# Issuing every TensorE product as four products of 32 output columns

## The chip, the core and the metric

The kernel runs on one core of a Trainium2 chip. The metric is the device time of the program in microseconds (us). Two runs of the kernel before gave 811.21 and 811.91 us, median 811.56 us. TensorE is PE in the profile, its weight loads are PEld, VectorE is DVE, ScalarE is ACT, GpSimd is POOL, SyncE is SP.

## What is computed

Eight sequences of 512 tokens with 128 features pass through one transformer-like block: a layer norm modulated by a condition, two recurrences over the 512 tokens (a small state space with a silu, and a gated recurrent unit), a second layer norm, and a mixture of eight experts of which each token uses one.

```python
def step(carry, inp):                      # 512 times, one after the other
    h_ssm, h_rnn = carry
    bxt, dxt, gxt, iht = inp
    h_ssm = jax.nn.silu(h_ssm @ A.T + bxt)
    y_ssm = h_ssm @ Cw.T + Cb + dxt
    hh = h_rnn @ W_hh.T + b_hh
    i_r, i_z, i_n = jnp.split(iht, 3, axis=-1)
    h_r, h_z, h_n = jnp.split(hh, 3, axis=-1)
    r = jax.nn.sigmoid(i_r + h_r)
    z = jax.nn.sigmoid(i_z + h_z)
    n = jnp.tanh(i_n + r * h_n)
    h_rnn = (1.0 - z) * n + z * h_rnn
    y_rnn = h_rnn @ proj_w.T + proj_b
    fused = gxt[:, :1] * y_ssm + gxt[:, 1:2] * y_rnn
    return ((h_ssm, h_rnn), fused)
...
for e in range(8):                         # expert of a token: argmax of its gate
    ye = jax.nn.relu(x @ w1[e] + b1[e]) @ w2[e] + b2[e]
    out = out + jnp.where(expert_idx == e, ye * expert_w, 0.0)
```

Everything is float32, apart from a few exact bfloat16 helpers (counts of tokens per expert, and the bias of the output in three bfloat16 parts).

## The kernel before

The features lie on the 128 partitions. The 512 tokens of a sequence are 512 steps; 16 steps of the eight sequences make a tile of 128 tokens, so there are 32 tiles. Each engine has one long program, written out step by step in Python (`steps`, up to U_END), and the engines meet through semaphores; nothing reorders the work at run time apart from these waits.

A step g on TensorE (`step`, L1276) is, in this order: the product of W_hh for r with the state h (L1287, 16 moving columns of which 8 are used), the one for n (L1291, 32 columns), the one for z (L1296, 16 columns). I call these three the narrow products. Then comes what the step has of the tile's other work (`tile_work`, L1232: output, router, token counts, input products), up to two units of the experts (`unit`, L1182), or, where a step has room, a product whose result nobody reads (`hold_clock`, L1177, 128 or 256 columns), and last the product of the state space (L1168, widened to 128 columns, of which 8 are used). I call all with 128 or more moving columns wide. In the 512 steps there are 1536 narrow products, 1237 wide float32 products of 128 (or 130) columns, 62 of 256, 113 transposes, 62 bfloat16 products of 128 columns and 31 of 258 (the bias); behind the last step there are 200 wide products and 16 transposes more, for the last tile and the remaining experts.

The first narrow product waits for h (`h_ready`), which is on every other engine's path: ACT takes the sigmoid of r from PSUM (L685), DVE forms i_n + r * h_n as a scan (L1015, waits for r's sigmoid and for n's product), ACT takes the tanh (L709), DVE forms the new h with another scan (L1023), and h_ready goes up again.

In float32 each product is issued as two passes of a weight load and a matmul (the trace has 1024 of each for 512 products); a transpose is one pass. The bias product L1241 has three rows (`ones_tok = ones_bf[0:KB, :]`, KB = 3), all others 128.

Of the kernel before, what the change touches and what calls it, by code (L numbers as in the profile page):

```python
# [17 lines left out]
BF16 = mybir.dt.bfloat16  # L18
I32 = mybir.dt.int32
U32 = mybir.dt.uint32  # L20
ALU = mybir.AluOpType
# [3 lines left out]
P = 128  # L25
# [6 lines left out]
EPS = 1e-5  # L32
BANK = 512
R_WIDE, N_WIDE, Z_WIDE, S_WIDE = 16, 32, 16, 128
HW = 32


KB = 3
# [50 lines left out]
RING = 12  # L89
# [117 lines left out]
def adaln_kernel(nc, x, silu_in, weights, ssm_weights, w1, b1, w2, b2, col_bias, bias_a, bias_b,  # L207
                 bias_const, const, out):
    ctx = ExitStack()
    with ctx:  # L210
# [27 lines left out]
        part_b = sb("part_b", [KB, BI_ALL], BF16)  # L238
        bias_bf = sb("bias_bf", [KB, BI_ALL], BF16)
        ones_bf = sb("ones_bf", [P, P], BF16)  # L240
# [211 lines left out]
        ident = const_sb[:, C_ID:C_ID + P]  # L452
        ones_tok = ones_bf[0:KB, :]

# [87 lines left out]
        def _(eng):  # L542
# [7 lines left out]
            eng.memset(s_ring[:, 1, T - 1, :], 0.0).then_inc(state_zeroed, 1)  # L550
            eng.memset(s_ring[:, 0, :, :], 0.0).then_inc(state_zeroed, 1)
            nc.gpsimd.iota(order_i[:, :], [[1, P]], base=0, channel_multiplier=-1).then_inc(iota_set, 1)
            nc.gpsimd.iota(count_i[:, :], [[1, 16]], base=0, channel_multiplier=0).then_inc(iota_set, 1)
# [216 lines left out]
        def _(eng):  # L770
# [83 lines left out]
            nc.vector.memset(ones_e[:, :], 1.0).then_inc(tables_set, 1)  # L854
            eng.wait_ge(state_zeroed, 7)

            def bias_part(n):


                if n == 0:  # L860
                    eng.wait_ge(bias_loaded, 48)
                    nc.vector.tensor_tensor(part_f[:, :], ba_sb[:, :], bb_sb[:, :], ALU.add).then_inc(bias_step, 1)
                    return
                eng.wait_ge(bias_step, n)
                k, what = divmod(n - 1, 3)
                mask = bc_sb[:, k:k + 1]
                if what == 0:
                    nc.vector.tensor_copy(part_b[:, :], part_f[:, :]).then_inc(bias_step, 1)
                if what == 1 and k == 0:
                    nc.vector.tensor_scalar(bias_bf[:, :], part_b[:, :], mask, None, ALU.mult).then_inc(bias_step, 1)  # L870
                if what == 1 and k > 0:
                    nc.vector.scalar_tensor_tensor(out=bias_bf[:, :], in0=part_b[:, :], scalar=mask,
                                                   in1=bias_bf[:, :], op0=ALU.mult, op1=ALU.add).then_inc(bias_step, 1)
                if what == 2:
                    nc.vector.tensor_tensor(part_f[:, :], part_f[:, :], part_b[:, :],
                                            ALU.subtract).then_inc(bias_step, 1)
# [241 lines left out]
        def _(eng):  # L1118
            mm = nc.tensor.matmul

# [14 lines left out]
            def pre(j, q, part):  # L1135

                if part == 0:
                    ge(eng, h1_ready, j + 1)
                    nc.tensor.transpose(work[:, 0:P], h1[:, :], ident).then_inc(h1T_filled, 1)
                if part == 1:  # L1140
# [21 lines left out]
            for part in range(1, 5):  # L1162
                pre(0, 0, part)
            eng.wait_ge(state_zeroed, 7)

# [16 lines left out]
            def unit(kind, i, second):  # L1182
# [6 lines left out]
                if kind == "X":  # L1189
# [7 lines left out]
                    else:  # L1197
                        ge(eng, h_ready, NT * T)
                    nc.tensor.transpose(rows_bank(n), xs_sb[:, b, :], ident).then_inc(x_filled, 1)  # L1199
                    return  # L1200
# [31 lines left out]
            def tile_work(c, q, t, g):  # L1232
# [3 lines left out]
                if exists(j):  # L1236
# [14 lines left out]
                    if t == 9:  # L1251
                        ge(eng, h2_ready, j + 1)
                        if exists(c + 1):
                            ge(eng, h1T_ready, c + 2)
                        nc.tensor.transpose(work[:, 0:P], h2_ring[:, j % RING, :], ident).then_inc(h2T_filled, 1)
                    if t == 10:
# [122 lines left out]
```

## Time and profile before

| | |
|---|---|
| time, median of 2 runs | 811.56 us |
| the profiled execution, its span | 825.0 us |
| PE busy, PEld busy | 799.6 us (97%), 754.8 us (91%) |
| DVE, ACT, POOL busy | 447.4, 388.8, 128.0 us |
| passes on PE | 6316 |
| granted TensorE clock, mean | 0.987 |

All terms of the prediction are made against the profiled execution, whose span is 13.4 us longer than the median. A busy PE is one with a matmul record open; such records overlap and their ends are modelled, so that PE's 97% doesn't tell whether PE is what the others wait for. The groups of rows further down show the step at close range.

### The profile page before, as it was taken

How to read it: one execution, taken by the hardware profiler on the slowest of the kernel's cores; microseconds unless marked ns; L12 is line 12 of the kernel's file. 1: busy time of each engine (PE TensorE's matmuls, PEld its weight loads, DVE VectorE, ACT ScalarE, POOL GpSimd, SP SyncE). 2: the span in 40 equal slices, each digit the busy share in tenths (PEclk: the TensorE clock that was granted, in tenths of full speed). 3: DMA queues.
4: the chain of work that ended last, by engine and by line, in shares of the span. 5: the costliest groups of instructions: out<-in, count | busy, mean ns of one | idle time of the engine just before them, and what ended most of it. 6: DMA issues, size and time to landing. Idle time of an engine off the chain costs nothing.

```text
span 825.0 us, 20239 instructions
## 1 busy us (share of the span) xinstructions
PE 799.6 (97%) x6316; PEld 754.8 (91%) x6316; DVE 447.4 (54%) x2715; ACT 388.8 (47%) x2689; POOL 128.0 (16%) x218
## 2 busy tenths in 40 slices
PE   8999999999999999999999999999999999998496
PEld 6999999999999999999999999999999999997486
DVE  5444444455555555555555556555556555656255
ACT  5444444444555444455555454555545555543132
POOL 2001111111110101111111111111111111212502
PEclk9999999999999999999999999999999999999789
DMA  8723000505322000062221002522200442215521
GB/s 315 277 86 123 6 4 5 207 6 194 108 76 71 11 11 11 25 224 106 68 67 50 11 11 78 206 81 82 81 14 18 147 140 88 84 60 208 202 64 46
DMA packets 45404, 75.72 MB, mean 92 GB/s; under 512 B 6284, under 2 KB 27090, under 8 KB 45170
## 3 DMA queue, kind: packets, MB, share of 16 engines
q1 hardware_dynamic: 41058, 68.40, 23.2%
q0 software_dynamic: 2368, 4.85, 2.1%
q10 hardware_dynamic: 1872, 1.18, 0.5%
q8 instruction: 51, 0.84, 0.4%
q14 instruction: 55, 0.45, 0.2%
HBM read 14.31 MB, written 21.04 MB: 43 GB/s over the span
## 4 chain that ended last, share of the span: by engine, by line
PE 95%; another core or an unknown queue 2%; DVE 1%; issue 1%; DMA 0%; ACT 0%; ACTq 0%; DVEq 0%
PE s_bank L1168 15%; PE nr_bank L1291 15%; PE nr_bank L1287 14%; PE z_bank L1296 13%; PE y_bank L1222 9%; PE hid_bank_b L1180 7%; PE hid_bank_a L1209 5%; PE hid_bank_b L1209 4%; PE work L1243 2%; PE nr_bank L1143 1%; PE s_bank L1155 1%; PE work L1258 1%; PE work L1246 1%; PE hid_bank_a L1199 1%; PE z_bank L1151 1%
## 5 line engine op out<-in xcount | busy, mean ns | idle before, releaser
L685 ACT ACTIVATE r_fac<-nr_bank 128x8 f32<-128x8 f32 x512 | 91.3, 178 | 280.1 <-PE nr_bank L1287 277.2
L1015 DVE TENSOR_TENSOR_SCAN nr_bank<-r_fac,nr_bank 128x16 f32<-128x16 f32 x512 | 100.0, 195 | 205.8 <-PE nr_bank L1291 201.2
L1168 PE MATMUL s_bank<-s_ring,ws_sb 128*128 128x128 f32 x1024 | 207.0, 284 | 0.0
L1291 PE MATMUL nr_bank<-h_ring,w_sb 128*128 128x32 f32 x1024 | 199.8, 279 | 0.0
L1296 PE MATMUL z_bank<-h_ring,w_sb 128*128 128x16 f32 x1024 | 191.6, 263 | 0.0
L1287 PE MATMUL nr_bank<-h_ring,w_sb 128*128 128x16 f32 x1024 | 184.9, 256 | 0.0
L1287 PEld LDWEIGHTS nr_bank<-h_ring,w_sb 128*128 128x128 f32 x1024 | 152.4, 188 | 22.2 <-DVE h_ring L1023 13.6
L1023 DVE TENSOR_TENSOR_SCAN h_ring<-z_fac,h_ring 128x24 f32<-128x24 f32 x512 | 106.5, 208 | 119.5 <-ACT h_ring L709 106.9
L1168 PEld LDWEIGHTS s_bank<-s_ring,ws_sb 128*128 128x128 f32 x1024 | 158.2, 190 | 7.1 <-issue 1.9
L1296 PEld LDWEIGHTS z_bank<-h_ring,w_sb 128*128 128x128 f32 x1024 | 155.5, 192 | 0.0
L1291 PEld LDWEIGHTS nr_bank<-h_ring,w_sb 128*128 128x128 f32 x1024 | 155.5, 192 | 0.0
L707 ACT ACTIVATE z_fac<-z_bank 128x8 f32<-128x8 f32 x512 | 92.6, 181 | 88.1 <-PE z_bank L1296 85.8
L562 POOL TENSOR_TENSOR ve<-mv,eps 128x1 f32<-128x1 f32 x64 | 12.0, 187 | 517.6 <-DVE mv L787 517.6
L709 ACT ACTIVATE h_ring<-nr_bank 128x16 f32<-128x16 f32 x512 | 92.2, 180 | 0.1
L691 ACT ACTIVATE s_fac<-s_bank 64x8 f32<-64x8 f32 x512 | 81.1, 158 | 0.4 <-PE s_bank L1168 0.4
L1180 PE MATMUL hid_bank_b<-w_sb,const_sb 128*128 128x128 f32 (+1 forms) x286 | 76.2, 348 | 0.0
L1019 DVE TENSOR_TENSOR s_ring<-s_bank,s_fac 64x8 f32<-64x8 f32 x512 | 75.6, 148 | 1.0
L1209 PE MATMUL hid_bank_a<-xT,wx 128*128 128x128 f32 x264 | 57.4, 300 | 9.5 <-issue 5.5
L678 ACT ACTIVATE hid_a<-hid_bank_a,wx 128x128 f32<-128x128 f32 x132 | 48.2, 365 | 30.6 <-PE hid_bank_a L1209 19.8
L1209 PE MATMUL hid_bank_b<-xT,wx 128*128 128x128 f32 x264 | 56.7, 298 | 2.4 <-DVE hid_b L1081 2.3
L1222 PE MATMUL y_bank<-wx,hid_a 128*128 128x128 f32 x264 | 56.2, 295 | 0.5 <-DVE y_sb L1093 0.5
L1222 PE MATMUL y_bank<-wx,hid_b 128*128 128x128 f32 x264 | 56.4, 296 | 0.0
(182 smaller groups left out, 1105.1 us busy)
## 6 DMA issues: line engine op xcount, KB each, us to landing
wx<-w_all SPq DMA_DIRECT2D x66, 578.0 KB
rows<-zeros SPq DMA_DIRECT2D x3, 4096.0 KB, 13.9
w_all<-in_w SPq DMA_DIRECT2D x2, 2048.0 KB, 15.5
xs_sb<-rows SPq DMA_DIRECT2D x54, 64.0 KB, 2.5
rows<-y_sb SPq DMA_DIRECT2D x54, 64.0 KB, 1.6
x_sb<-in_x SPq DMA_DIRECT2D x1, 1920.0 KB, 8.8
out<-o_sb SPq DMA_DIRECT2D x20, 64.0 KB
y_rows<-y_sb SPq DMA_DIRECT2D x12, 64.0 KB, 1.8
```

What stands on the lines that cost most here:

```text
L685: nc.scalar.activation(r_fac[:, t % 2, :, 1], r_cols(q, t), ACT.Sigmoid).then_inc(rn_ready, 1)
L707: nc.scalar.activation(z_fac[:, t % 2, :, 2], z_cols(g), ACT.Sigmoid).then_inc(sig_ready, 1)
L709: nc.scalar.activation(scan_data(pq, pt).rearrange("p (b m) -> p b m", m=3)[:, :, 0:3:2], n_pairs(q, t)[:, :, 1:2].to_broadcast([P, B, 2]) ...
L1015: nc.vector.tensor_tensor_scan(pairs, r_fac[:, k, :, :].rearrange("p b k -> p (b k)"), pairs, 0.0, ALU.mult, ALU.add).then_inc(pre_n_ready, 1)
L1023: nc.vector.tensor_tensor_scan(h_ring[:, q, t, 0:3 * B], z_fac[:, k, :, :].rearrange("p b m -> p (b m)"), scan_data(pq, pt), 0.0, ALU.mult ...
L1168: return mm(s_cols(g, width=S_WIDE), ws_sb[:, 0:P], s_ring[:, pq, pt, :], start=False, stop=True, skip_group_check=True)
L1180: mm(hid_bank[1][:, 0:width], ident, w_sb[:, W_MOD:W_MOD + width], start=True, stop=True)
L1209: mm(hid_bank[second][:, 0:P], w_all[:, e, at:at + P] if dense else wx1[:, b, at:at + P], h2T[:, (NT - 1) % 2, :] if dense else xT[:, n % ...
L1222: last = mm(dense_y(e) if dense else y_bank[:, 0:P], (hid_a, hid_b)[second][:, h, :], w_all[:, e, FC * P + at:FC * P + at + P] if dense el ...
L1287: mm(r_cols(q, t, R_WIDE), w_sb[:, W_HH:W_HH + P], h[:, 0:R_WIDE], start=False, stop=True, skip_group_check=True).then_inc(r_ready, 1)
L1291: mm(n_pairs(q, t, N_WIDE)[:, :, 0], w_sb[:, W_HH + 2 * P:W_HH + 3 * P], h[:, 0:N_WIDE], start=False, stop=True, skip_group_check=True).th ...
L1296: mm(z, w_sb[:, W_HH + P:W_HH + 2 * P], h[:, 0:z.shape[1]], start=False, stop=True, skip_group_check=True).then_inc(z_ready, 1)
```

## The change

TensorE's program no longer calls the matmul directly. A helper `mm` cuts the stationary operand into four pieces of 32 columns and issues four products, each into 32 partitions of the output, with the same moving operand; a semaphore is raised by the last of the four. The transposes become products of the tile (as weights) with the identity (as moving operand), through the same helper, and so have two passes per piece. The bias operand gets all 128 partitions, zero but for the first three, and the ones beside it too, so that the bias product has 128 rows as all others have. One memset on POOL at the start is added, and the waits for it.

```diff
--- before.py
+++ after.py
@@ -31,6 +31,7 @@
 FC = 4
 EPS = 1e-5
 BANK = 512
+COLS = 32
 R_WIDE, N_WIDE, Z_WIDE, S_WIDE = 16, 32, 16, 128
 HW = 32
 
@@ -236,7 +237,7 @@
         bc_sb = sb("bc_sb", [KB, KB])
         part_f = sb("part_f", [KB, BI_ALL])
         part_b = sb("part_b", [KB, BI_ALL], BF16)
-        bias_bf = sb("bias_bf", [KB, BI_ALL], BF16)
+        bias_bf = sb("bias_bf", [P, BI_ALL], BF16)
         ones_bf = sb("ones_bf", [P, P], BF16)
         ct_sb = sb("ct_sb", [P, B])
         ct_sig = sb("ct_sig", [P, B])
@@ -450,7 +451,7 @@
 
         mod_sa, mod_ca, mod_ga, mod_sb, mod_cb, mod_gb = (mod[:, k * P:(k + 1) * P] for k in range(6))
         ident = const_sb[:, C_ID:C_ID + P]
-        ones_tok = ones_bf[0:KB, :]
+        ones_tok = ones_bf[:, :]
 
         block = ctx.enter_context(nc.Block())
 
@@ -549,6 +550,7 @@
             eng.memset(z_fac[:, :, :, 1], -1.0).then_inc(state_zeroed, 1)
             eng.memset(s_ring[:, 1, T - 1, :], 0.0).then_inc(state_zeroed, 1)
             eng.memset(s_ring[:, 0, :, :], 0.0).then_inc(state_zeroed, 1)
+            eng.memset(bias_bf[:, :], 0.0).then_inc(state_zeroed, 1)
             nc.gpsimd.iota(order_i[:, :], [[1, P]], base=0, channel_multiplier=-1).then_inc(iota_set, 1)
             nc.gpsimd.iota(count_i[:, :], [[1, 16]], base=0, channel_multiplier=0).then_inc(iota_set, 1)
             nc.gpsimd.iota(block_i[:, :], [[P, E * GMAX]], base=0, channel_multiplier=0).then_inc(iota_set, 1)
@@ -852,7 +854,7 @@
                                            op0=ALU.add, op1=ALU.mult).then_inc(mod_ready, 1)
             nc.vector.memset(ones_bf[:, :], 1.0).then_inc(ones_set, 1)
             nc.vector.memset(ones_e[:, :], 1.0).then_inc(tables_set, 1)
-            eng.wait_ge(state_zeroed, 7)
+            eng.wait_ge(state_zeroed, 8)
 
             def bias_part(n):
 
@@ -867,10 +869,10 @@
                 if what == 0:
                     nc.vector.tensor_copy(part_b[:, :], part_f[:, :]).then_inc(bias_step, 1)
                 if what == 1 and k == 0:
-                    nc.vector.tensor_scalar(bias_bf[:, :], part_b[:, :], mask, None, ALU.mult).then_inc(bias_step, 1)
+                    nc.vector.tensor_scalar(bias_bf[0:KB, :], part_b[:, :], mask, None, ALU.mult).then_inc(bias_step, 1)
                 if what == 1 and k > 0:
-                    nc.vector.scalar_tensor_tensor(out=bias_bf[:, :], in0=part_b[:, :], scalar=mask,
-                                                   in1=bias_bf[:, :], op0=ALU.mult, op1=ALU.add).then_inc(bias_step, 1)
+                    nc.vector.scalar_tensor_tensor(out=bias_bf[0:KB, :], in0=part_b[:, :], scalar=mask,
+                                                   in1=bias_bf[0:KB, :], op0=ALU.mult, op1=ALU.add).then_inc(bias_step, 1)
                 if what == 2:
                     nc.vector.tensor_tensor(part_f[:, :], part_f[:, :], part_b[:, :],
                                             ALU.subtract).then_inc(bias_step, 1)
@@ -1116,7 +1118,16 @@
 
         @block.tensor
         def _(eng):
-            mm = nc.tensor.matmul
+            def mm(out, weights, moving, start, stop, skip_group_check=False):
+
+                for c in range(0, P, COLS):
+                    last = nc.tensor.matmul(out[c:c + COLS], weights[:, c:c + COLS], moving, start=start, stop=stop,
+                                            skip_group_check=skip_group_check)
+                return last
+
+            def transpose(out, tile):
+
+                return mm(out, tile, ident, start=True, stop=True)
 
 
             def fill(filled):
@@ -1136,7 +1147,7 @@
 
                 if part == 0:
                     ge(eng, h1_ready, j + 1)
-                    nc.tensor.transpose(work[:, 0:P], h1[:, :], ident).then_inc(h1T_filled, 1)
+                    transpose(work[:, 0:P], h1[:, :]).then_inc(h1T_filled, 1)
                 if part == 1:
                     ge(eng, n_seeded, 2 * j + 2)
                     ge(eng, h1T_ready, j + 1)
@@ -1161,7 +1172,7 @@
             eng.wait_ge(w_loaded, 48)
             for part in range(1, 5):
                 pre(0, 0, part)
-            eng.wait_ge(state_zeroed, 7)
+            eng.wait_ge(state_zeroed, 8)
 
             def state_space(g, pq, pt):
 
@@ -1196,7 +1207,7 @@
                         ge(eng, relu_a_ready, 2 * i)
                     else:
                         ge(eng, h_ready, NT * T)
-                    nc.tensor.transpose(rows_bank(n), xs_sb[:, b, :], ident).then_inc(x_filled, 1)
+                    transpose(rows_bank(n), xs_sb[:, b, :]).then_inc(x_filled, 1)
                     return
                 if kind in "AC":
                     if kind == "A" and not second:
@@ -1252,7 +1263,7 @@
                         ge(eng, h2_ready, j + 1)
                         if exists(c + 1):
                             ge(eng, h1T_ready, c + 2)
-                        nc.tensor.transpose(work[:, 0:P], h2_ring[:, j % RING, :], ident).then_inc(h2T_filled, 1)
+                        transpose(work[:, 0:P], h2_ring[:, j % RING, :]).then_inc(h2T_filled, 1)
                     if t == 10:
                         ge(eng, h2T_ready, j + 1)
                         mm(work[:, 0:P], h2T[:, jq, :], repeated(w_sb[:, W_ROUTE:W_ROUTE + E]),
```

What stands on PE's queue, in the order of the program. First, the second step of the second tile and most of the third, as an example of the loop: h_ring is the state h, nr_bank and z_bank take the gates, hid_bank_b takes the product that keeps the clock or an expert's hidden layer, s_bank the state space. Before:

```order
L1287 MATMUL nr_bank<-h_ring,w_sb 128x16
L1291 MATMUL nr_bank<-h_ring,w_sb 128x32
L1296 MATMUL z_bank<-h_ring,w_sb 128x16
L1246 MATMUL work<-w_sb,h_hist 128x128
L1249 MATMUL work<-ws_sb,s_hist 128x128
L1168 MATMUL s_bank<-s_ring,ws_sb 128x128
L1287 MATMUL nr_bank<-h_ring,w_sb 128x16
L1291 MATMUL nr_bank<-h_ring,w_sb 128x32
L1296 MATMUL z_bank<-h_ring,w_sb 128x16
L1180 MATMUL hid_bank_b<-w_sb,const_sb 128x256
```

The same place with the change:

```order
L1124 MATMUL nr_bank<-h_ring,w_sb 32x16 x4
L1124 MATMUL nr_bank<-h_ring,w_sb 32x32 x4
L1124 MATMUL z_bank<-h_ring,w_sb 32x16 x4
L1124 MATMUL work<-w_sb,h_hist 32x128 x4
L1124 MATMUL work<-ws_sb,s_hist 32x128 x4
L1124 MATMUL s_bank<-s_ring,ws_sb 32x128 x4
L1124 MATMUL nr_bank<-h_ring,w_sb 32x16 x4
L1124 MATMUL nr_bank<-h_ring,w_sb 32x32 x4
L1124 MATMUL z_bank<-h_ring,w_sb 32x16 x4
L1124 MATMUL hid_bank_b<-w_sb,const_sb 32x256 x4
```

No product changes its place; each has become four in a row, all of them issued by the helper's line 1124, with 32 output partitions instead of 128 and the same number of moving columns.

The other place is the first step of that tile, where the bias product stands (bias_bf, into the bank work). Before:

```order
L1296 MATMUL z_bank<-h_ring,w_sb 128x16
L1241 MATMUL work<-bias_bf,ones_bf 128x258
L1243 MATMUL work<-w_sb,h1T 128x130
L1168 MATMUL s_bank<-s_ring,ws_sb 128x128
L1287 MATMUL nr_bank<-h_ring,w_sb 128x16
```

With the change:

```order
L1124 MATMUL z_bank<-h_ring,w_sb 32x16 x4
L1124 MATMUL work<-bias_bf,ones_bf 32x258 x4
L1124 MATMUL work<-w_sb,h1T 32x130 x4
L1124 MATMUL s_bank<-s_ring,ws_sb 32x128 x4
L1124 MATMUL nr_bank<-h_ring,w_sb 32x16 x4
```

Here too the order stays, and the bias product has 32 columns and 128 rows like its neighbours.

## Rows read from the trace of the kernel before

**Rows 1.** The page: busy time of each engine, and the granted clock over the span.

```profile
PE 799.6 (97%) x6316; PEld 754.8 (91%) x6316; DVE 447.4 (54%) x2715; ACT 388.8 (47%) x2689; POOL 128.0 (16%) x218
...
PEclk9999999999999999999999999999999999999789
```

**Rows 2.** The line that makes h: count, ns min/median/max, first and last start.

```profile
L1023 DVE TENSOR_TENSOR_SCAN h_ring<-z_fac,h_ring x512: 207/208/210, 11.4 to 743.2; 128x24 f32<-128x24 f32 x171
```

**Rows 3.** Timeline of one step, all engines: start us, us, engine, line, instruction, count.

```profile
300.30 0.21 DVE L1023 TENSOR_TENSOR_SCAN h_ring<-z_fac,h_ring 128x24 f32<-128x24 f32 x1 [0.24 <-ACT h_ring L709]
...
300.56 0.30 PEld L1287 LDWEIGHTS nr_bank<-h_ring,w_sb 128*128 128x128 f32 x2
...
300.78 0.30 PEld L1291 LDWEIGHTS nr_bank<-h_ring,w_sb 128*128 128x128 f32 x2
...
300.99 0.18 ACT L685 ACTIVATE r_fac<-nr_bank 128x8 f32<-128x8 f32 x1 [0.73 <-PE nr_bank L1287]
301.00 0.30 PEld L1296 LDWEIGHTS z_bank<-h_ring,w_sb 128*128 128x128 f32 x2
...
301.23 0.20 DVE L1015 TENSOR_TENSOR_SCAN nr_bank<-r_fac,nr_bank 128x16 f32<-128x16 f32 x1 [0.39 <-PE nr_bank L1291]
...
301.51 0.18 ACT L709 ACTIVATE h_ring<-nr_bank 128x16 f32<-128x16 f32 x1
...
301.73 0.21 DVE L1023 TENSOR_TENSOR_SCAN h_ring<-z_fac,h_ring 128x24 f32<-128x24 f32 x1 [0.24 <-ACT h_ring L709]
...
301.99 0.30 PEld L1287 LDWEIGHTS nr_bank<-h_ring,w_sb 128*128 128x128 f32 x2
```

**Rows 4.** Who waited for whom during the 512 steps: total us, times, longest.

```profile
ACT r_fac L685 <- PE nr_bank L1287: 276.4, 491, 0.8
DVE nr_bank L1015 <- PE nr_bank L1291: 200.1, 437, 0.9
...
PEld nr_bank L1287 <- DVE h_ring L1023: 13.6, 89, 0.2
```

**Rows 5.** Groups of TensorE instructions by shape: count, busy us, mean ns, idle before.

```profile
L1168 PE MATMUL s_bank<-s_ring,ws_sb 128*128 128x128 f32 x1024 | 207.0, 284 | 0.0
...
L1296 PE MATMUL z_bank<-h_ring,w_sb 128*128 128x16 f32 x1024 | 191.6, 263 | 0.0
...
L1255 PE MATMUL work<-const_sb,h_ring 128*128 128x128 f32 x32 | 9.8, 308 | 0.1
```

**Rows 6.** Timeline of weight loads around a 256-column product.

```profile
24.13 0.41 PEld L1168 LDWEIGHTS s_bank<-s_ring,ws_sb 128*128 128x128 f32 x2
```

**Rows 7.** Timeline of matmuls at the same place.

```profile
23.82 0.68 PE L1180 MATMUL hid_bank_b<-w_sb,const_sb 128*128 128x256 f32 x2
24.34 0.38 PE L1168 MATMUL s_bank<-s_ring,ws_sb 128*128 128x128 f32 x2
```

**Rows 8.** Timeline of matmuls around the two bfloat16 products of a tile.

```profile
76.78 0.22 PE L1264 MATMUL work<-onehot,before 128*128 128x128 bf16 x1
76.84 0.22 PE L1266 MATMUL work<-onehot,ones_bf 128*128 128x128 bf16 x1
76.90 0.44 PE L1180 MATMUL hid_bank_b<-w_sb,const_sb 128*128 128x128 f32 x2
```

**Rows 9.** Timeline of weight loads around the three-row bias product.

```profile
79.39 0.30 PEld L1296 LDWEIGHTS z_bank<-h_ring,w_sb 128*128 128x128 f32 x2
79.72 0.09 PEld L1241 LDWEIGHTS work<-bias_bf,ones_bf 3*128 3x128 bf16 x1
79.93 0.30 PEld L1243 LDWEIGHTS work<-w_sb,h1T 128*128 128x128 f32 x2
```

**Rows 10.** Stretches of the steps and behind them: length, busy us (count), clock.

```profile
11.40:743.20 731.80, 731.41 (x5868) 695.84 (x5868) 401.40 (x2543) 357.94 (x2602) 100.02 (x174) 1.00 0.24 85
743.20:825.00 81.80, 59.12 (x422) 54.24 (x421) 39.59 (x148) 23.23 (x72) 23.75 (x26) 0.87 0.38 131
```

**Rows 11.** The page: PE's instruction fetches, and a 64 KB transfer from issue to landing.

```profile
q8 instruction: 51, 0.84, 0.4%
...
xs_sb<-rows SPq DMA_DIRECT2D x54, 64.0 KB, 2.5
```

## The prediction

> **What bounds the kernel now.** I began with the page [rows 1]: PE has a matmul open in 97% of the span and its clock is full until the last few slices, which looks like a kernel bound by TensorE. The rest says otherwise. The line that makes h runs 512 times, first at 11.4 and last at 743.2 us [rows 2]: (743.2 - 11.4) / 511 = 1.432 us a step, in steps that hold quite different products. One step at close range [rows 3] is a ring: h's scan starts at 300.30, r's first weight load at 300.56 (0.26 later), the sigmoid of r at 300.99 (0.43), the scan for n at 301.23 (0.24), tanh at 301.51 (0.28), h's next scan at 301.73 (0.22): 1.43 us, all of it one after the other. ACT and DVE wait in it for the products of r and n, and PE's next load of r for h, if only by 13.6 us in all [rows 4].
>
> So two things have nearly the same length. The ring takes 1.43 us. PE's own work per step is six products at 0.22 us (the loads of r, n and z start at 300.56, 300.78, 301.00 [rows 3]), 1.34 us with 0.224 each. The other stretches matter less: 11.4 us before the first h, and 81.8 us behind the last, of which PE is busy 59.1 [rows 10].
>
> **What sets 0.22 us.** Products of 16 and of 128 moving columns have the same pace, two loads at 0.11 us each, so for the narrow ones the load is what counts: 0.112 for 128 weight columns. Streaming shows where 256 columns move: the next product's loads begin when the last such pass starts (24.13 [rows 6]), and its first matmul starts at 24.34 [rows 7], so 256 columns stream in 0.21 to 0.22 us and 128 in 0.109. A wide product is thus bound twice over, by loading and by streaming, at about the same 0.11 us a pass.
>
> **Loads after the change.** Four pieces of two passes make eight loads per product. In proportion to its columns a load of 32 takes 0.028 us, eight 0.224, as now. No row shows a load of fewer than 128 columns, nor two at once. The lower bound is that the four pieces load side by side, two loads in a row, 0.056 a product. The upper bound comes from the densest stream there is, the bfloat16 pair: matmuls start at 76.78, 76.84, 76.90 [rows 8], each with its load, so a load and a matmul are certainly issued every 0.056 us, 0.448 a product. I take 0.224, as the rate per column is the only thing measured. The Trainium skill, TensorEngine Tiling, section Instruction Overhead, says that each matmul costs about 60 cycles however few columns move; as an estimate from that page this is 25 ns, 0.2 us per narrow product, and the sum below would be about 37 us less. No row here decides between the two.
>
> **Streaming after the change.** This is the largest term. The moving operand isn't cut, so each of the eight passes streams all its columns: 0.109 us for 128. The lower bound is that the four pieces run fully side by side: two passes in a row, 0.22 us, as now. The upper bound is that none overlaps: 8 x 0.109 = 0.872. I take a value between, from the order on the queue. The pieces are issued one after the other, and each as its first pass, then its second. The second pass of a piece needs the same 32 columns of the array as the first, so it starts when that one has streamed. PE starts matmuls in the order of the program in all timelines read; if it keeps to that, the first pass of piece two waits behind the second of piece one, and then runs beside it. So at most two passes run at once, and a product takes four passes, 4 x 0.109 = 0.436 us. The Trainium skill, TensorE: Matmul & The Clock Gate, section The mechanism, also says that matmuls start strictly in order. The same page's table of measured speedups has three column tiles of one pass each at 2.38 times; an estimate with that, 0.872 / (4 x 0.79) = 0.276 us a wide product, would give about 850 us, but it has no second pass on the same tile, which is what I expect to block.
>
> **The sum.** In the 512 steps, by the counts of the program: 1536 narrow products x 0.224 = 344 us; wide ones, 1237 of 128 columns, 113 transposes (one pass now [rows 5], full products then) and 62 of 256 as two each, 1474 x 0.436 = 643; bfloat16 products 7. Together 994 us. No step falls below the ring: with three wide products it has 3 x 0.224 + 3 x 0.436 = 1.98 us on PE against 1.43, and steps with any other mix of the same size are alike. PE is then the bound, and ring waits vanish inside it. Now the 512 steps take 732, so +262. Behind them 200 wide products gain 0.212 each and 16 transposes 0.324, 47 us; PE's idle 22.7 us of that stretch [rows 10] are waits for other engines, and I let all 47 stand. Before the first step the wide fills and input products double, some 4 us. The span becomes 825 + 262 + 47 + 4 = 1138 us; the median stood 13.4 us below its span, so **1125 us**.
>
> Costed at nothing: the memset on POOL lies before 4 us, while POOL next waits for DVE. The bias product now makes PE pause: loads start 79.72 and 79.93 around it, the last load before at 79.50 [rows 9], some 0.2 us of idle in 31 steps, 6 us at most, and with PE the bound this is a gain that its four pieces, streaming 258 columns, eat. Instruction fetches quadruple from 51 [rows 11]; the queue runs ahead of them now without a mark in the steps. If each of some 153 new ones stood free for as long as a small transfer, 2.5 us [rows 11], that would be 380 us, but one is needed only every 5 us.
>
> If the queue order holds but narrow products reach half my price, 0.112, the steps take 172 + 643 + 7 = 822 and the time is about 950. So the likeliest case has its own range, 950 to 1190.
>
> **The rivals.**
> *Faster: the pieces run side by side.* If a blocked second pass doesn't hold up the next piece, a wide product stays at 0.224. If loads overlap too, a narrow one falls to 0.112, the wait from r's load to its sigmoid from 0.43 to 0.32, and n's product is earlier still. The ring is 0.112 shorter, PE needs 6 x 0.17 = 1.01 us, and 512 x 0.112 = 57 us go: 755 us, or 725 with loads of 0.056. For it: the ring is what counts now, and its PE part is nearly half load time. Against it: the order of the passes. It decides from the point where three narrow and three wide products fit 1.43 us; at 0.436 the wide ones alone take 1.31.
> *No change: streaming side by side, loads as now.* Narrow 0.224, wide 0.224, the ring and PE as before: about 812 us. The change then does nothing.
> *Slower through issue.* If each load with its matmul costs 0.056 us whatever its size [rows 8], every product takes 0.448: 688 + 660 + 7 in the steps, with the tail about 1490 us. Against it: that spacing is also just the streaming of 128 bfloat16 columns.
> *Much slower: no overlap at all.* Wide 0.872: steps 344 + 1285 + 7 = 1636, with the tail about 1860 us. For it: the trace shows no two matmuls of pieces at once. Against it: pieces use different columns and output partitions.
>
> **How the numbers follow.** Queue order, 1125 us (950 to 1190): 0.54. Faster, 755: 0.18. No change, 812: 0.10. Issue, 1490: 0.08. No overlap, 1860: 0.10. The range of 725 to 1200 leaves out the last two, about 2 in 10, and takes in both signs, since the bounds of the wide product decide the sign. A measurement of this kernel tells about 2% from no change. Faster by more than 2%: 0.18; within 2%: 0.10; slower: 0.72.
>
> **What would show it.** In the profile after: the state space product's eight passes spread over 0.44 us, with neighbours starting in pairs; PE without waits in the loop; and ACT's sigmoid and DVE's scans waiting longer for PE at each step, about 1.9 us from one h to the next. The narrow price shows in the starts of r, n and z: 0.22 apart if loads are proportional, 0.11 or less if they overlap. I am wrong if wide products take 0.25 us or less: then the ring decides again, and the sign with it. The tail term is wrong if the stretch behind the last h isn't about 130 us.

## The result, and the profile after

Two runs of the changed kernel took 850.01 and 859.72 us, median 854.87 us, against 811.56 before: ratio 1.053, 95% interval 1.039 to 1.068. It is slower, as forecast, and inside the range, but it loses 43 us and not 313.

The profiled execution took 850.01 us, with a span of 847.9. The page: the first line gives busy time, share of the span and instructions of each engine, the second the granted clock in 40 slices, the third PE's instruction fetches (count, MB, share of the transfer engines).

```profile
PE 706.2 (83%) x25784; PEld 466.4 (55%) x25784; DVE 446.4 (53%) x2715; ACT 405.0 (48%) x2689; POOL 127.9 (15%) x219
...
PEclk9998999899999999999999999999999999999999
...
q8 instruction: 203, 3.33, 1.6%
```

PE is less busy than before (83% against 97% [rows 1]) in a longer span. Something other than PE's work holds it. The one figure that has quadrupled along with the passes is the count of instruction fetches, 51 [rows 11] to 203. 3.33 MB over 203 fetches is 16.4 KB each. PE's queue has 2 x 25784 loads and matmuls and some 530 waits for semaphores, 52095 records in all, and over 203 that is 256.6: a fetch brings some 256 instructions. I call 256 instructions a block.

The line that makes h (L1025 now), with the times of its first and last scan:

```profile
L1025 DVE TENSOR_TENSOR_SCAN h_ring<-z_fac,h_ring x512: 207/208/210, 11.7 to 777.1; 128x24 f32<-128x24 f32 x171
```

(777.1 - 11.7) / 511 = 1.498 us a step, against 1.432 [rows 2]. That is the mean. The typical step is another matter. One step at close range (start, length, engine, line, operation, out<-in, count, idle time before it and what ended that):

```profile
311.90 0.21 DVE L1025 TENSOR_TENSOR_SCAN h_ring<-z_fac,h_ring 128x24 f32<-128x24 f32 x1 [0.20 <-ACT h_ring L711]
...
312.16 0.22 PEld L1124 LDWEIGHTS nr_bank<-h_ring,w_sb 128*32 128x32 f32 x16 [0.25 <-DVE h_ring L1025]
...
312.28 0.18 PEld L1124 LDWEIGHTS z_bank<-h_ring,w_sb 128*32 128x32 f32 x8
...
312.49 0.18 ACT L687 ACTIVATE r_fac<-nr_bank 128x8 f32<-128x8 f32 x1 [0.62 <-PE nr_bank L1124]
...
312.70 0.20 DVE L1017 TENSOR_TENSOR_SCAN nr_bank<-r_fac,nr_bank 128x16 f32<-128x16 f32 x1 [0.52 <-ACT r_fac L687]
...
312.93 0.19 ACT L711 ACTIVATE h_ring<-nr_bank 128x16 f32<-128x16 f32 x1
...
313.01 0.42 PE L1124 MATMUL s_bank<-s_ring,ws_sb 128*32 128x128 f32 x8
...
313.15 0.21 DVE L1025 TENSOR_TENSOR_SCAN h_ring<-z_fac,h_ring 128x24 f32<-128x24 f32 x1 [0.20 <-ACT h_ring L711]
```

From scan to scan it takes 1.25 us, where the ring of before took 1.43 [rows 3]. From r's load to its sigmoid it is 0.33 us (0.43 before), from the sigmoid to the scan for n 0.21 (0.24), from there to tanh 0.23 (0.28). The sixteen loads of r and n together start within 0.12 us, 0.06 a product, where one took 0.22.

The state-space product has eight passes, each with 128 moving columns. The matmuls of that product alone, in two stretches, 312.99 to 313.12 and 312.99 to 313.16 (count, shortest/median/longest ns, first and last start):

```profile
L1124 PE MATMUL s_bank<-s_ring,ws_sb x4: 297/297/297, 313.0 to 313.0; 128*32 128x128 f32 x4
...
L1124 PE MATMUL s_bank<-s_ring,ws_sb x8: 272/285/297, 313.0 to 313.2; 128*32 128x128 f32 x8
```

Four passes are under way by 313.03 and nothing more starts until after 313.13; then the other four start within 0.03 us. In the trace's single records, neighbours within each four start some 7 ns apart. So all four pieces stream at once, and a wide product costs two passes in a row, as before.

So the ring did become shorter. A typical step, by which I mean the tenth percentile of the 511 times from scan to scan, takes 1.243 us against 1.427 before; the median, 1.292, already holds delays. So 512 x 0.184 = 94 us should have gone. Here is one place where they went, weight loads a little later:

```profile
313.41 0.22 PEld L1124 LDWEIGHTS nr_bank<-h_ring,w_sb 128*32 128x32 f32 x16 [0.25 <-DVE h_ring L1025]
313.53 0.12 PEld L1124 LDWEIGHTS z_bank<-h_ring,w_sb 128*32 128x32 f32 x1
314.50 0.15 PEld L1124 LDWEIGHTS z_bank<-h_ring,w_sb 128*32 128x32 f32 x7 [0.85 <-issue]
```

One of z's eight loads goes out, and the next seven come 0.97 us later, with no semaphore behind it ("issue" is waiting for nothing the profile shows). In the transfer records an instruction fetch runs from 311.97 to 313.31, and the next starts at 315.76. The stop lies inside a product, where the program has no wait. In PE's waits (total us, times, longest) such stops are spread over all its tiles:

```profile
PEld nr_bank L1124 <- issue: 40.8, 50, 3.2
...
PEld z_bank L1124 <- issue: 28.0, 37, 4.0
...
PEld s_bank L1124 <- issue: 21.0, 34, 2.1
...
PEld hid_bank_a L1124 <- issue: 14.7, 27, 1.5
...
PEld y_bank L1124 <- issue: 10.8, 15, 1.4
...
PEld hid_bank_b L1124 <- issue: 9.8, 9, 2.1
...
PEld work L1124 <- issue: 9.1, 13, 1.5
```

These seven rows are 134 us, 124 of them in the steps. The steps together exceed 512 typical ones by 130 us; before, by 2.6. Counting PE's instructions through, waits included, 133 of its 324 gaps over 0.35 us stand at one and the same place modulo 256, and no other place has more than 5.

The single records settle what these 133 stops wait for. Blocks and fetches pair one to one, 203 and 203. At the 133 places PE goes on 1.39 us (median; nine in ten between 1.24 and 1.57) behind the end of the fetch that brings the block. The next fetch starts only after PE has entered that block, 1.04 us later at the least and 1.23 in the median. And of the 130 us, 116 lie in the 228 steps that touch the end of a block, 10 in the steps right behind these, and 4.6 in the other 95.

The two stretches, with the columns of [rows 10] (length, busy us and count of PE, PEld, DVE, ACT, POOL, clock, DMA share, GB/s):

```profile
11.70:777.10 765.40, 638.92 (x23913) 414.86 (x23916) 400.48 (x2542) 374.26 (x2601) 99.56 (x174) 0.98 0.25 84
777.10:847.90 70.80, 57.44 (x1748) 47.98 (x1745) 39.50 (x148) 23.13 (x72) 23.82 (x26) 0.94 0.45 154
```

The steps cost 765.4 - 731.8 = 33.6 us more. The rest behind them took 81.8 us in the profiled execution of before. That execution had a span of 825.0; a time lies 2.1 above its span (850.01 and 847.9), so the median of 811.56 belongs to a span of 809.4, and the profiled one was 15.6 longer. Its steps ran undisturbed at full clock and its tail at 0.87 [rows 10], so I put the 15.6 to the tail. Without them it has 66.2, and the tail becomes about 4.6 us longer with the change, an estimate. The start went from 11.4 to 11.7.

**The theory.** The pieces overlap fully, and the ring gives back 94 us. But in the steps PE now has 94.5 instructions each, 93.6 of them loads and matmuls (23.9 before), so 256 of them last 256 / 94.5 x 1.243 = 3.37 us at the ring's pace, and the next 256 take about 4 us to come. I call this *fetch*. The rival, *work*, says that the extra passes themselves, or the waits among them, make some steps longer, wherever they lie in the fetch blocks.

### The profile page after: what moved, and what is told of

The parts are those of the page before. It is cut to its first block, busy times and chain, and to the rows that moved or that the text cites. A ratio compares the mean times of both kernels' runs of the same rounds, so it can differ in the third digit from the quotient of the medians.

```text
span 847.9 us, 59176 instructions
## 1 busy us (share of the span) xinstructions
PE 706.2 (83%) x25784; PEld 466.4 (55%) x25784; DVE 446.4 (53%) x2715; ACT 405.0 (48%) x2689; POOL 127.9 (15%) x219
## 3 DMA queue, kind: packets, MB, share of 16 engines
q8 instruction: 203, 3.33, 1.6%
## 4 chain that ended last, share of the span: by engine, by line
PE 71%; issue 14%; DVE 6%; ACT 5%; DMA 1%; SPq 1%; POOL 0%; DVEq 0%; POOLq 0%
PE s_bank L1124 23%; PE nr_bank L1124 19%; PE hid_bank_b L1124 8%; PE work L1124 6%; PE y_bank L1124 6%; PE hid_bank_a L1124 5%; PE z_bank L1124 4%; ACT r_fac L687 3%; DVE nr_bank L1017 3%; DVE s_ring L1021 1%; DMA out<-o_sb 1%; ACT h_ring L711 0%; DMA xs_sb<-rows,x_index 0%; ACT s_bank L658 0%; DVE fin_g L1101 0%
## 5 line engine op out<-in xcount | busy, mean ns | idle before, releaser
L1124 PE MATMUL s_bank<-s_ring,ws_sb 128*32 128x128 f32 x4096 | 236.1, 287 | 29.6 <-DVE s_ring L1021 16.1
L1124 PE MATMUL nr_bank<-h_ring,w_sb 128*32 128x16 f32 (+1 forms) x8192 | 203.5, 202 | 31.5 <-issue 30.1
L1124 PEld LDWEIGHTS nr_bank<-h_ring,w_sb 128*32 128x32 f32 x8192 | 144.1, 112 | 114.1 <-DVE h_ring L1025 76.8
L1124 PEld LDWEIGHTS s_bank<-s_ring,ws_sb 128*32 128x32 f32 x4096 | 104.6, 110 | 140.0 <-DVE s_ring L1021 107.1
L1025 DVE TENSOR_TENSOR_SCAN h_ring<-z_fac,h_ring 128x24 f32<-128x24 f32 x512 | 106.3, 208 | 115.1 <-ACT h_ring L711 114.0
L1124 PE MATMUL z_bank<-h_ring,w_sb 128*32 128x16 f32 x4096 | 142.3, 191 | 20.4 <-issue 20.2
L1124 PEld LDWEIGHTS z_bank<-h_ring,w_sb 128*32 128x32 f32 x4096 | 106.8, 118 | 26.5 <-issue 26.5
L1124 PE MATMUL hid_bank_b<-w_sb,const_sb 128*32 128x128 f32 (+1 forms) x1144 | 79.8, 335 | 2.3 <-issue 2.3
L1124 PE MATMUL hid_bank_b<-xT,wx 128*32 128x128 f32 x1056 | 60.4, 281 | 6.1 <-issue 5.5
L1124 PE MATMUL hid_bank_a<-xT,wx 128*32 128x128 f32 x1056 | 59.9, 284 | 3.9 <-issue 3.7
L1124 PE MATMUL y_bank<-wx,hid_a 128*32 128x128 f32 x1056 | 59.7, 277 | 3.7 <-issue 3.4
L680 ACT ACTIVATE hid_a<-hid_bank_a,wx 128x128 f32<-128x128 f32 x132 | 48.0, 364 | 19.9 <-PE hid_bank_a L1124 19.5
```

The lines of the kernel that those rows point to most:

```text
L680: nc.scalar.activation(hid_a[:, h, :], hid_bank[0][:, 0:P], ACT.Relu, bias=bias1(i, 2 * h)).then_inc(relu_a_ready, 1)
L1025: nc.vector.tensor_tensor_scan(h_ring[:, q, t, 0:3 * B], z_fac[:, k, :, :].rearrange("p b m -> p (b m)"), scan_data(pq, pt), 0.0, ALU.mult ...
L1124: last = nc.tensor.matmul(out[c:c + COLS], weights[:, c:c + COLS], moving, start=start, stop=stop, skip_group_check=skip_group_check)
```

## The experiments

Numbers in the table are worked out from the h scans and from the counts of PE's instructions in the steps (loads, matmuls and 0.9 waits a step). "Typical step" is the tenth percentile of the time from scan to scan, "excess" what the steps take beyond as many typical ones, whatever the reason; "block at ring pace" is 256 / (instructions per step) x (typical step), "block measured" the time from first to last scan over the number of blocks in it.

| kernel | time, us | ratio (95%) | typical step | mean step | instr. per step | block at ring pace | block measured | excess, us |
|---|---|---|---|---|---|---|---|---|
| before | 811.56 | – | 1.427 | 1.432 | 23.9 | 15.3 | 15.4 | 3 |
| after, 32 columns | 854.87 | 1.053 (1.039–1.068) | 1.243 | 1.498 | 94.5 | 3.37 | 4.06 | 130 |
| 64 columns | 737.27 | 0.908 (0.906–0.910) | 1.263 | 1.287 | 47.7 | 6.78 | 6.91 | 12 |
| state space 2 of 4 | 805.25 | 0.992 (0.989–0.996) | 1.242 | 1.407 | 86.5 | 3.68 | 4.16 | 84 |
| narrow ones only | 772.66 | 0.950 (0.944–0.956) | 1.255 | 1.359 | 59.9 | 5.36 | 5.81 | 53 |
| 16 passes added | 964.42 | 1.192 (1.184–1.199) | 1.244 | 1.718 | 110.5 | 2.88 | 3.98 | 242 |
| zeros written later | 849.18 | 1.045 (1.043–1.047) | 1.243 | 1.512 | 94.5 | 3.37 | 4.10 | 137 |
| state space 2 of 4, no fill | 785.54 | 0.969 (0.964–0.973) | 1.242 | 1.376 | 82.1 | 3.87 | 4.29 | 68 |
| 64, lean state space | 730.52 | 0.901 (0.899–0.903) | 1.263 | 1.277 | 43.7 | 7.40 | 7.48 | 7 |

### Half as many pieces: 64 columns

```diff
-COLS = 32
+COLS = 64
```

> Pieces of 64 columns instead of 32: half the instructions of the changed kernel on PE (about 26 thousand against 52). Fetch theory (PE stops at every 256th instruction until the next block of instructions has come, about 4 us after the one before): a block then lasts over five steps, 6.9 us, no stop is left, and the ring of a step is 1.24 us plus 0.056 for the two longer loads of r, 1.30 us: 512 x 1.30 + 82 = about 750 us. Work theory (the pieces themselves cost PE time, or the clock that drops in the stops): halving the pieces takes back half of the loss, about 830 us.

737.27 us, ratio 0.908. This is the test with the most in it: the same mechanism of pieces, half the instructions. The page and PE's waits for issue:

```profile
PE 706.1 (96%) x12892; PEld 532.6 (72%) x12892; DVE 443.7 (60%) x2715; ACT 422.4 (57%) x2689; POOL 128.1 (17%) x219
...
q8 instruction: 102, 1.67, 0.9%
```

```profile
PEld s_bank L1124 <- issue: 6.0, 19, 0.3
...
PEld hid_bank_a L1124 <- issue: 5.9, 15, 0.6
...
PEld nr_bank L1124 <- issue: 2.6, 6, 0.6
```

The loss through issue is down to an eighth, 17 us in all rows, where the kernel before has 16. The typical step is only 0.02 us longer than with 32 columns, so nearly all of the ring's gain is there already. The 12 us of excess that are left aren't stops: the steps at place 5 of a tile's 16 take 1.32 us and those at 11 to 13 1.29 (medians).

### Half of the state-space pieces left out

The product of the state space writes 128 partitions, of which the state uses the first 64; the two pieces behind are left out.

```diff
-            def mm(out, weights, moving, start, stop, skip_group_check=False):
+            def mm(out, weights, moving, start, stop, skip_group_check=False, cols=P):
-                for c in range(0, P, COLS):
+                for c in range(0, cols, COLS):
...
-                          start=False, stop=True, skip_group_check=True)
+                          start=False, stop=True, skip_group_check=True, cols=SSM)
```

> The changed kernel, but the state space product (64 outputs used, 128 columns issued) issues only the two pieces whose result is read: 8 instructions less per step, 4096 in all, 16 blocks of 256; nothing that is used is left out. Fetch theory: 16 blocks x 4.05 us = about 65 us less, 790 us. Work theory: the four pieces run side by side, so two take as long as four: no change, 850 to 855 us.

805.25 us, 50 less than after. The product's pieces stream at once, so its duration is the same with two, and the typical step is indeed unchanged (1.242). What fell is the instructions, by 8 a step, 16 blocks in the steps: 50 / 16 = 3.1 us a block. That is a good deal of the 4 us expected, and nothing that *work* allows.

### Sixteen instructions added to each step

```diff
+                mm(s_cols(g), ws_sb[:, 0:P], zeros[:, 0:B], start=False, stop=True, skip_group_check=True)
                 return mm(s_cols(g, width=S_WIDE), ws_sb[:, 0:P], s_ring[:, pq, pt, :],
```

The added product adds zeros, in the stretch of the step in which PE waits for the state anyway.

> The changed kernel plus one product of 8 moving columns of zeros per step, added to the state space bank in front of its product: 16 instructions more per step, 8192 in all, 32 blocks; results are unchanged. Fetch theory: 32 x 4.05 us = 130 us more, about 985 us. Work theory: PE has 0.06 us more to do in a step in which it idles a sixth of the time: 855 to 885 us.

964.42 us, 110 more than after, for 8 matmuls of 8 columns with their loads. The typical step doesn't move (1.244). Loads and matmuls in the steps grow by 32 blocks, 3.4 us each. PE's waits:

```profile
PEld s_bank L1124 <- issue: 61.1, 75, 4.7
PEld nr_bank L1124 <- issue: 58.8, 68, 2.4
...
PEld z_bank L1124 <- issue: 38.7, 35, 3.8
```

Each of the three has grown (21.0, 40.8 and 28.0 in after), the products of r and z too, which the edit doesn't touch. The added instructions cost where the block ends, not where they stand. *Work* falls with this run and the one before.

### Only the three narrow products in pieces

Made from the kernel before, with a helper `pieces` like `mm` of the change; all other products stay whole.

```diff
-                    mm(r_cols(q, t, R_WIDE), w_sb[:, W_HH:W_HH + P], h[:, 0:R_WIDE],
+                    pieces(r_cols(q, t, R_WIDE), w_sb[:, W_HH:W_HH + P], h[:, 0:R_WIDE],
...
-                    mm(n_pairs(q, t, N_WIDE)[:, :, 0], w_sb[:, W_HH + 2 * P:W_HH + 3 * P], h[:, 0:N_WIDE],
+                    pieces(n_pairs(q, t, N_WIDE)[:, :, 0], w_sb[:, W_HH + 2 * P:W_HH + 3 * P], h[:, 0:N_WIDE],
...
-                    mm(z, w_sb[:, W_HH + P:W_HH + 2 * P], h[:, 0:z.shape[1]],
+                    pieces(z, w_sb[:, W_HH + P:W_HH + 2 * P], h[:, 0:z.shape[1]],
```

> The kernel before, with only the three narrow products of a step in four pieces; all others, transposes and the three-row bias product too, as before. 31 thousand PE instructions, so by the fetch theory no stop is left. Then what shows is the price of changing between pieces and whole products twice a step. If a change costs nothing, the ring is that of the changed kernel, 1.24 us, and the time about 720 us. If each costs 0.2 us as around the three-row bias product of before, PE needs 0.3 + 0.2 + 0.67 + 0.2 = 1.37 us a step: about 785 us, more if the second change falls on the ring.

772.66 us, ratio 0.950. The ring's gain needs only the three narrow products, and 59.9 instructions a step stay clear of the 4 us. But over a quarter of the steps take about 1.48 us, while most take 1.255, and it isn't the fetch: steps that touch the end of a block are no longer than others (medians 1.259 and 1.260). Nor is it the number of wide products, as two of three steps with three of them take about 1.26 us. 122 of the 147 steps over 1.45 us stand at places 5 and 11 to 13 of a tile. There PE has a product of the next tile beside the one of the state space (11 to 13), or the state space's product waits for its bank (5), and r's load comes 0.50 us behind the start of h's scan, where it comes 0.28 behind it in other steps. Weight loads of a usual step, and then the end of a step at place 11, with h's scan:

```profile
451.28 0.22 PEld L1125 LDWEIGHTS nr_bank<-h_ring,w_sb 128*32 128x32 f32 x16
451.40 0.18 PEld L1125 LDWEIGHTS z_bank<-h_ring,w_sb 128*32 128x32 f32 x8
451.61 0.30 PEld L1254 LDWEIGHTS work<-w_sb,h_hist 128*128 128x128 f32 x2
```

```profile
26.93 0.30 PEld L1176 LDWEIGHTS s_bank<-s_ring,ws_sb 128*128 128x128 f32 x2 [0.21 <-DVE s_ring L1020]
...
27.08 0.21 DVE L1024 TENSOR_TENSOR_SCAN h_ring<-z_fac,h_ring 128x24 f32<-128x24 f32 x1 [0.20 <-ACT h_ring L710]
27.15 0.30 PEld L1155 LDWEIGHTS nr_bank<-h1T,w_sb 128*128 128x128 f32 x2
...
27.57 0.22 PEld L1125 LDWEIGHTS nr_bank<-h_ring,w_sb 128*32 128x32 f32 x16
```

In the first, z's loads begin at 451.40 and the first whole load comes 0.21 us later, where the next product follows z's after 0.09 us when it is in pieces too (in after, 312.28 to 312.37). In the second, a whole product follows another after 0.22 us (26.93 to 27.15), but r's pieces follow a whole one after 0.42, although h's scan ended at 27.29. Each change between pieces and whole thus costs 0.1 to 0.2 us, two a step. In most steps h comes no earlier than PE is through with the change; at the four places it does, and with 64 columns, where nothing changes, the same places take 1.29 to 1.32 us instead of 1.48. These 122 steps make about 27 of the 53 us of excess; the rest I did not take apart. The Trainium skill, TensorEngine Tiling, section Key Properties, says that changing the tiling mode drains the engine; it gives no price, and the trace agrees with about 0.2 us at most a change.

### The long transfers moved

Zeros are written to two large buffers in tiles 2 and 6; here in tiles 4 and 10. Nothing else changes.

```diff
-                if t == 0 and c in (2, 6):
+                if t == 0 and c in (4, 10):
-                    zero_rows(1 if c == 2 else 2)
+                    zero_rows(1 if c == 4 else 2)
```

> The changed kernel with the two 4 MB transfers that zero row buffers moved from the start of tiles 2 and 6 to the start of tiles 4 and 10. In the changed kernel the 16 steps of tiles 2, 4, 6, 10 take 26.3, 22.4, 27.3, 23.9 us. If instruction fetches are slowed by bulk transfers, the long tiles move along: about 22, 27, 22.5, 28 us, the time unchanged, 855 us. If the long tiles have another reason (what is computed in them), they stay where they are.

849.18 us: total within what two runs of after leave open, but the long tiles have moved. Stretches of tiles 2, 4, 6 and 10 in after, with the columns of the stretches above:

```profile
63.63:89.95 26.32, 21.14 (x722) 13.88 (x719) 11.12 (x74) 10.84 (x78) 2.68 (x5) 0.87 0.46 166
...
112.45:134.86 22.41, 19.59 (x721) 11.69 (x718) 11.02 (x74) 10.78 (x78) 2.61 (x5) 1.00 0.03 7
...
156.41:183.72 27.31, 21.34 (x721) 13.97 (x718) 11.02 (x73) 10.83 (x78) 2.61 (x5) 0.88 0.43 159
...
254.71:278.62 23.91, 20.59 (x778) 13.57 (x782) 12.68 (x80) 12.21 (x85) 2.61 (x5) 1.00 0.21 71
```

And with the zeros in tiles 4 and 10:

```profile
65.06:86.83 21.77, 19.82 (x722) 11.25 (x718) 11.08 (x73) 10.81 (x78) 2.68 (x5) 1.00 0.03 8
...
108.54:133.77 25.23, 20.33 (x721) 13.12 (x719) 11.01 (x74) 11.04 (x78) 2.61 (x5) 0.93 0.47 172
...
155.88:177.50 21.62, 19.22 (x722) 12.00 (x718) 11.02 (x74) 10.72 (x78) 2.61 (x5) 1.00 0.03 7
...
248.99:280.42 31.43, 22.64 (x778) 17.43 (x775) 12.73 (x81) 12.40 (x85) 2.61 (x5) 0.84 0.53 194
```

Tile 6 goes from 27.3 to 21.6 us as its transfers leave, tile 10 from 23.9 to 31.4 as they come, with the same count of matmuls. So fetches come later where bulk transfers run. Yet a quiet tile at full clock takes 21.6 to 22.4 us, and 16 x 1.243 is 19.9: without any transfer the steps would lose some 2 us a tile, an estimate of 50 to 80 us of the 130 over 32 tiles. Inside tile 2 of after, three stretches of 5 us, one in the burst and two behind it:

```profile
70.00:75.00 5.00, 2.76 (x68) 1.64 (x61) 1.68 (x9) 1.37 (x12) 0.76 (x1) 0.81 1.02 369
75.00:80.00 5.00, 4.75 (x158) 4.13 (x161) 1.94 (x12) 1.90 (x13) 0.75 (x2) 0.66 0.06 20
80.00:85.00 5.00, 4.60 (x200) 3.00 (x192) 2.51 (x18) 2.36 (x20) 0.00 (x0) 1.00 0.03 7
```

PE gets through 68 matmuls while the transfers move 369 GB/s, and through 200 later. The granted clock falls to its lower level, 1.2 GHz, behind that starved stretch (0.66 from 75 to 80), and the two steps that start there take 1.69 and 1.60 us, the next three 1.25. The clock is thus part of the loss, and it follows the stops: the steps have 0.98 on average, against 1.00 before [rows 10]. The trace bounds its share. 30 steps touch the lower level and hold 30 of the 130 us; the 15 of them that touch no end of a block take 1.61 us on average, 0.36 more than a typical step. At that price the clock's own part is about 11 us, an estimate, and most of the rest is stops.

### Fewer instructions with 32 columns: no fill

The 143 products that only keep the clock and whose results nobody reads are left out, on top of the run with half of the state-space pieces.

```diff
-                ge(eng, relu_b_ready, count_of("AC", u, place))
-                mm(hid_bank[1][:, 0:width], ident, w_sb[:, W_MOD:W_MOD + width], start=True, stop=True)
+                return
```

> Pieces of 32 columns; the state space product with two pieces, and the 143 products that nobody reads (they keep TensorE busy) left out: 6384 instructions less than the changed kernel, 25 blocks of 256. Fetch theory: at 3.1 to 3.5 us a block, as between this kernel's neighbours with two and with six pieces more, about 80 us less than the changed kernel, 775 us. Theory that only PE idle in the right place matters: the products left out lie in PE's idle time, so no gain over the kernel with two pieces, 805 us, or a loss where the clock falls.

785.54 us, 20 less than with the fill, and about 10 more than expected. The block takes 4.29 us. Without the fill the mean clock is 0.938; at one stretch near the start it stays at its lower level for 37.5 us. The gain was probably paid back in part there, so this run supports the direction and not the size.

### A version that beats both

64 columns, the state-space product as one piece of 64 output columns, and only 32 moving columns in it.

```diff
-COLS = 32
-R_WIDE, N_WIDE, Z_WIDE, S_WIDE = 16, 32, 16, 128
+COLS = 64
+R_WIDE, N_WIDE, Z_WIDE, S_WIDE = 16, 32, 16, 32
...
-                          start=False, stop=True, skip_group_check=True)
+                          start=False, stop=True, skip_group_check=True, cols=SSM)
```

(`mm` has `cols` as in the run with two of four.)

> Pieces of 64 columns, the state space product with only the one piece whose result is read and 32 moving columns instead of 128 (8 are used): nothing that is used is left out. In the run with 64 columns most steps take 1.26 us, but those with the most products 1.29 to 1.46, mean 1.287 us. If PE's streaming is what lengthens those, 0.16 us less of it per step brings the mean to 1.265 us: 512 x 0.022 = 11 us less, about 726 us. If the narrower product lets the granted clock fall, no gain or a loss: 737 us or more.

730.52 us, ratio 0.901, 124 us better than the change. The page, and the shares of the chain of work that ended last, by engine:

```profile
PE 662.6 (91%) x11868; PEld 520.1 (71%) x11868; DVE 442.5 (61%) x2715; ACT 421.3 (58%) x2689; POOL 126.7 (17%) x219
...
q8 instruction: 94, 1.54, 0.9%
...
PE 36%; DVE 27%; ACT 24%; issue 9%; DMA 2%; DVEq 0%; POOL 0%; POOLq 0%
```

The chain goes round the ring's three engines, as it should. Mean and typical step are 0.014 us apart; what is left is the ring. Of the 11 us that were expected against 64 columns alone, 7 came: places 5 and 11 to 13 of a tile now take 1.264 us. Whether the piece left out or the narrower moving operand did it wasn't separated.

## Why the prediction was right in sign and wrong in size

**The bound before: right.** The ring of 1.43 us bound the steps, and PE's work per step lay close below. The runs in pieces confirm it: shorten the part of the ring that lies on PE, and the typical step follows, to 1.243.

**The price of a wide product: wrong, and the largest miss.** The step that failed is that "the first pass of piece two waits behind the second of piece one". It gave 0.436 us. The trace shows four starts, then four more about 0.13 us behind: 0.22 to 0.26 us, the lower bound I named. Of 643 us for wide products in the steps 40 to 50% was too much. I had named 0.25 us or less as the sign of being wrong, after which the ring would decide again and the sign with it. The ring did become the bound of an undisturbed step, but the sign stayed, for a reason that stands further down. The records don't say which pass of which piece a start is, so whether the hardware or the order on the queue avoids the block stays open; in either case the array ran four matmuls at once. The Trainium skill, TensorE: Matmul & The Clock Gate, section The mechanism, has tiles that run at the same time, which this trace confirms, and it was my own step from "in order" to "the next piece waits" that was wrong. The estimate from that page's speedup came to about 850 us and so lay near the time; but it got there with longer wide products and a bound on PE, and neither is in the trace.

**The price of a narrow product: wrong.** I took 0.224 us, loads in proportion to their columns and one after the other. Loads of different pieces overlap: 0.06 to 0.09 us a product, near the lower bound of 0.056. The estimate of 25 ns a matmul from the Trainium skill, TensorEngine Tiling, section Instruction Overhead, isn't borne out as a limit on starts across pieces, which are 7 ns apart here.

**The ring: the "faster" rival was right about it.** It put the wait from r's load to its sigmoid at 0.32 us (measured 0.33), and its lower end, 725 us, is near what the change would have given without stops: the profiled execution's 850 less the 130 us of excess is 720. The scan for n and tanh came earlier too, by 0.08 together.

**The instruction fetches: costed at nothing, and they decided the sign.** I wrote that a new fetch "is needed only every 5 us" and held against that 2.5 us, the time of a small transfer. Both figures failed. The 5 us belongs to steps of 1.9 to 2 us, as the sum had them, and with the true 1.243 it is 3.37. And a block takes about 4 us to follow the one ahead: fetch starts lie 3.3 us apart at the least, with a median of 3.83, and the mean grows from 3.8 us where other transfers move under 50 GB/s to 5.1 at 200 to 400. The fetch's own packets take 1.0 to 1.1 us in any case; what I left out are the 1.4 us from its end to PE's next instruction, and that it starts over 1 us after PE has entered the block before. The two errors are linked: with steps as slow as predicted, the fetch would mostly have stayed hidden (an estimate: 256 instructions in 5.3 us, against the 3.8 to 5.1 above), and a faster ring is what brought it out.

**The tail and the start.** +47 us was predicted behind the last h, a stretch of about 130 us; it took 70.8, about +5, since wide products didn't double. About 10 us of stops lie in it. The start's +4 was +0.3.

**The sum, corrected.** 811.6 - 94.0 (ring) + 127.7 (excess, beyond that of before) + 4.6 (tail) + 0.3 (start) = 850.2, and the profiled execution took 850.0; the other run, which has no trace, took 859.7. The sign was right for a wrong reason: "slower" in the forecast meant PE bound by streaming, and it is PE starved of instructions.

## What to carry to other kernels

Cutting a product into column pieces shortens the load of the weights and so a latency-bound ring, even if the moving operand streams as long as before. Count the instructions before choosing the width: divide 256 by the instructions of a step, multiply by the step's new length, and if less than about 4 us come out (more beside bulk transfers), the engine stops for its next block; here 64 columns with 6.9 us a block won 9%, 32 columns with 3.4 lost 5%. Cut everything on the engine, or keep pieces and whole products in long runs, as each change between them costs 0.1 to 0.2 us.

## What the runs showed that I had not expected

- A steady limit on PE's instructions: in all kernels whose ring asks for a block of 256 in under 3.9 us, the steps ran at 3.98 to 4.29 us a block, whatever the instructions were, products of 8 columns or of 128.
- The limit has three parts in after. From PE's entry into a block to the start of the next fetch it is 1.4 us on average where other transfers move under 50 GB/s, the fetch takes 1.1, and from its end to PE's next instruction it is 1.4 again (blocks that end in a stop).
- Bulk transfers slow this: at 369 GB/s, 68 matmuls in 5 us against 200 in a quiet stretch. Only the first of the three parts grows, to 2.7 us at 200 to 400 GB/s; the other two stay at 1.0 and 1.4. What holds the fetch back before it starts isn't in the trace and stays open.
- Four pieces' matmuls start some 7 ns apart, loads of r and n, sixteen in all, within 0.12 us.
- A change between pieces and whole products costs about 0.1 to 0.2 us of PE, at 451.40 to 451.61 and 27.15 to 27.57 in the run with only the narrow products cut.
